# A recurrent attention and feed-forward kernel: the pipeline over batches shortened by one stage, with another slot order on every engine

## The reference

```python
q, k, v = split(LN(x) @ W_qkv.T)            # per head
k = (k - mean(k)) / sqrt(var(k) + eps)
F_t = retention * F_{t-1} + coef * outer(v_t, k_t)   # per head, 16x16, over the tokens
y_t = (W_LTM + F_t) @ q_t
x1 = x + LN(y @ W_o.T)
h = relu(LN(x1) @ W_fc.T) ** 2              # 1024 features
y = h @ W_proj.T
s = share of 5 steps in which a leaky integrator driven by y spikes
out = x1 + LN(s)
```

## Time and profile before

| | |
|---|---|
| median of 3 runs | 677.21 us (675.97 to 677.54) |
| the profiled execution: its own time | 680.4 us |
| its span, first to last instruction | 678.6 us |
| busy: TensorE, VectorE, ScalarE, GpSimd | 515.4, 544.6, 334.3, 384.4 us |
| mean granted TensorE clock | 0.888 |

### The profile page before, as it was taken

The page is one execution under the profiler, slowest core; times in us unless marked ns, Lnnn a source line. Parts: engine busy times, 40 slices in busy tenths (PEclk is TensorE's granted clock), DMA queues, the critical chain, the costliest instruction groups (busy, mean ns, idle before and its releaser), DMA issues.

```text
span 678.6 us, 7833 instructions
## 1 busy us (share of the span) xinstructions
PE 515.4 (76%) x2256; PEld 335.9 (49%) x2256; DVE 544.6 (80%) x1022; ACT 334.3 (49%) x633; POOL 384.4 (57%) x181
## 2 busy tenths in 40 slices
PE   0438458468998779878996979887978797797791
PEld 0224224234665357635764557545744573375570
DVE  4558999999899988997899789979998999911101
ACT  2423112334645654665556465665556534666734
POOL 0235765587558755865677556766577556812101
PEclk9999697777998889979898979987997899799796
DMA  6155654564455336544555454536353464020000
GB/s 222 46 155 149 173 174 148 149 185 139 131 158 178 125 116 179 172 138 116 179 161 136 112 176 127 175 88 190 126 148 116 148 178 125 0 64 0 0 32 31
DMA packets 54458, 87.64 MB, mean 129 GB/s; under 512 B 5392, under 2 KB 19088, under 8 KB 54416
## 3 DMA queue, kind: packets, MB, share of 16 engines
q1 hardware_dynamic: 54416, 87.14, 43.3%
HBM read 78.74 MB, written 8.39 MB: 128 GB/s over the span
## 4 chain that ended last, share of the span: by engine, by line
PE 34%; issue 23%; DVE 18%; ACT 15%; POOL 9%; DMA 1%; SPq 0%; POOLq 0%; DVEq 0%; ACTq 0%
DVE state L665 10%; PE p_c L378 9%; POOL prod L790 8%; PE p_c L351 7%; PE p_a L283 6%; DVE p_u L655 4%; ACT sign L529 4%; PE p_c L339 3%; PE p_y L326 3%; PE p_c L360 3%; ACT oo L456 2%; PE p_a L303 2%; ACT spk L456 2%; DVE stats L619 1%; ACT hr L517 1%
## 5 line engine op out<-in xcount | busy, mean ns | idle before, releaser
L790 POOL TENSOR_TENSOR prod<-state,qf 128x1024 f32<-128x1024 f32 x128 | 302.8, 2369 | 179.4 <-DVE state L665 167.3
L665 DVE TENSOR_TENSOR_SCAN state<-ret,p_u 128x512 f32<-128x512 f32 x256 | 307.8, 1208 | 0.0
L655 DVE TENSOR_TENSOR p_u<-vrep,p_k 128x512 f32<-128x512 f32 x256 | 171.6, 676 | 22.2 <-ACT p_k L461 22.1
L283 PE MATMUL p_a<-xt,wqkv_s 128*128 128x512 f32 x288 | 98.4, 487 | 39.4 <-POOL xt L806 15.3
L351 PE MATMUL p_c<-wproj_sb,ht 128*128 128x256 f32 x512 | 118.5, 383 | 1.3 <-ACT ht L519 1.3
L351 PEld LDWEIGHTS p_c<-wproj_sb,ht 128*128 128x128 f32 x512 | 94.9, 190 | 29.7 <-issue 10.0
L378 PE MATMUL p_c<-x1t,wfc_s 128*128 128x512 f32 x384 | 106.5, 429 | 3.6 <-POOL x1t L806 2.4
L283 PEld LDWEIGHTS p_a<-xt,wqkv_s 128*128 128x128 f32 x288 | 64.6, 235 | 78.8 <-issue 23.0
L378 PEld LDWEIGHTS p_c<-x1t,wfc_s 128*128 128x128 f32 x384 | 77.7, 206 | 31.4 <-issue 10.6
L326 PE MATMUL p_y<-prod,summer 128*32 128x512 f32 x512 | 78.6, 690 | 5.2 <-POOL prod L790 5.2
L517 ACT ACTIVATE hr<-p_c 128x512 f32<-128x512 f32 x64 | 38.1, 595 | 47.7 <-PE p_c L378 45.6
(11 more groups left out here) (88 smaller groups left out, 502.3 us busy)
## 6 DMA issues: line engine op xcount, KB each, us to landing
vrep<-v_rows SPq DMA_DIRECT2D x256, 256.0 KB, 3.4
xa<-in_x SPq DMA_DIRECT2D x8, 512.0 KB, 4.7
v_rows<-vf SPq DMA_DIRECT2D x16, 256.0 KB, 3.4
x<-in_x SPq DMA_DIRECT2D x8, 512.0 KB, 4.2
out<-x SPq DMA_DIRECT2D x8, 512.0 KB, 3.1
prod<-in_w_fc SPq DMA_DIRECT2D x1, 1024.0 KB, 7.2
wproj_sb<-in_w_proj SPq DMA_DIRECT2D x1, 1024.0 KB, 9.4
state<-in_w_qkv SPq DMA_DIRECT2D x1, 768.0 KB, 5.6
```

The costliest lines, as they stand in the source:

```text
L283: last = pe.matmul(p_a[:, :], wqkv_s[:, i, t, first_col:first_col + P], xt[:, j, t, :], start=(t == i == j == 0), stop=(t == KT - 1 and i ...
L655: v.tensor_tensor(p_u[n % NU][:, :], vrep[:, n % NV, :], p_k[:, :], ALU.mult).then_inc(S["hebb_done"], 1)
L665: v.tensor_tensor_scan(state[:, s % NS, i, :], ret[:, r:r + 1].broadcast_to([P, L]), p_u[n % NU][:, :], 0.0, ALU.mult, ALU.add).then_inc(S ...
L790: p.tensor_tensor(prod[:, s % NZ, :, :], state[:, s % NS, :, :], qf[:, s // HS, :].unsqueeze(1).broadcast_to([P, 2, L]), ALU.mult).then_in ...
```

## The change

One of the three trailing iterations is dropped, and with it the stage g - 3. All eight ups and downs 0 and 1 of batch g - 1 now stand in iteration g; downs 2 and 3, signs, count, norm 4 and the last residual of batch g - 2 too. `down` is issued whole. Of the removed lines of the four `iteration` bodies only a part is shown; the kernel above has them.

```diff
--- before.py
+++ after.py
             iteration(B, False, True, True, False)
             iteration(B + 1, False, False, True, False)
-            iteration(B + 2, False, False, False, False)
...
                 for s in range(SLOTS):
                     spread_v(g, s)
                     if s == 4: store_v(g, 1)
-                    if s == 6 and g >= 3: store_out(g - 3)
-                    if s == 8 and g >= 1: load_again(g - 1)
+                    if s == 2 and g >= 3: store_out(g - 3)
+                    if s == 5 and g >= 1: load_again(g - 1)
                     if s == 13 and g < B - 1: store_v(g + 1, 0)
                     if s == 12 and g < B - 2: load_x(g + 2)
...
 
 
             def project_out(b, t):
-                pe.wait_ge(S["relu_done"], at(FT * b - 1 + t))
+                pe.wait_ge(S["yf_done"], at(TILES * (b - 1) + 3 + t))
                 pe.wait_ge(S["y_done"], at(2 * (b + 1)))
 
-            def down(b, u, part, next_too):
-                if part == 0:
-                    if u < 2:
-                        if u == 0: pe.wait_ge(S["h_done"], at(FT * (b + 1)))
-                        if next_too: pe.wait_ge(S["o_done"], at(2 * (b + 1) + u + 1))
-                    else:
-                        pe.wait_ge(S["yf_done"], at(TILES * b + u - 1))
-                for f in range(part * FT // 2, (part + 1) * FT // 2):
+            def down(b, u):
+                if u == 0: pe.wait_ge(S["h_done"], at(FT * (b + 1)))
+                if u >= 2: pe.wait_ge(S["yf_done"], at(TILES * b + u - 1))
+                for f in range(FT):
                     last = pe.matmul(p_c[(u + 1) % 2][:, 0:D], ht[:, f, tokens(u)], wproj_sb[:, f, :],
                                      start=(f == 0), stop=(f == FT - 1))
-                if part == 1:
-                    last.then_inc(S["down_done"], 1)
+                last.then_inc(S["down_done"], 1)
             def count_spikes(b, pair, next_too):
                 pe.wait_ge(S["sign_done"], at(2 * b + pair + 1))
                 if next_too: pe.wait_ge(S["x1t_done"], at(KT * (b + 1) + pair + 1))
+                else: pe.wait_ge(S["yf_done"], at(TILES * b + 3 + pair))
             def turn_x1(b, t):
                 pe.wait_ge(S["n3_done"], at(TILES * (b + 1)))
                 pe.wait_ge(S["o_done"], at(2 * (b + 1)))
-                pe.wait_ge(S["yf_done"], at(TILES * (b - 1) + 3 + t))
...
             def iteration(g, now, before, two_before, after):
                 b, b1, b2 = g + 1, g - 1, g - 2
                 for s in range(SLOTS):
-                    if before and s in (0, 2): sums(b1, 6 + s // 2)
+                    if before and s in (0, 1): sums(b1, 6 + s)
                     if now and s >= 4 and s % 2 == 0: sums(g, (s - 4) // 2)
...
                     if now:
                         if s == 0: project_v(g, 1)
                         if s == 1: project_k(g, 1)
                         if s == 2: key_variance(g, 1)
...
+                    if two_before and s in (0, 1): down(b2, 2 + s)
+                    if before and s == 2:
+                        project_out(b1, 0)
+                        project_out(b1, 1)
+                    if now and s == 3: project_q(g, 1)
                     if now and s == 5: key_scale(g, 1)
...
                     if after:
                         if s in (6, 7): turn_x(b, s - 6)
                         if s == 9: project_v(b, 0)
                         if s == 10: project_k(b, 0)
                         if s == 11: key_variance(b, 0)
...
+                        if s == 12: project_q(b, 0)
+                        if s == 13: key_scale(b, 0)
+                    if before and s == 8:
+                        turn_x1(b1, 0)
+                        turn_x1(b1, 1)
+                    if two_before and s == 9:
+                        count_spikes(b2, 0, before)
+                        count_spikes(b2, 1, before)
+                    if before and 9 <= s < 13:
+                        up(b1, 2 * (s - 9))
+                        up(b1, 2 * (s - 9) + 1)
+                    if before and s in (13, 14): down(b1, s - 13)
 
             run(iteration)
 
...
             nc.scalar.copy(wfc_s[:, 0, :, :], wfc_raw).then_inc(S["wide_high"], 1)
 
             def iteration(g, now, before, two_before, after):
...
+                b, b1, b2 = g + 1, g - 1, g - 2
                 for s in range(SLOTS):
...
+                    if s == 0:
+                        if now and before: copy_key(g, 0)
+                        if two_before: copy_yf(b2, 1)
+                        if now: copy_v(g, 1)
+                        if two_before: signs(b2, 0)
+                    if s == 1:
+                        if now: square_k(g, 1)
+                        if two_before: copy_yf(b2, 2)
+                    if s == 2:
+                        if before: copy_y(b1, 1)
+                        if two_before: copy_yf(b2, 3)
+                        if now: key_deviation(g, 1)
+                        if after: deviation(1, b)
+                        if before:
+                            copy_o(b1, 0)
+                            copy_o(b1, 1)
+                    if s == 3:
+                        if now: copy_q(g, 1)
+                        if after: norm1(b)
+                        if before: deviation(2, b1)
+                    if s == 4:
+                        if now: spread_k(g, 1)
+                        if before: norm(2, b1, oo, oo, "x1_done", b1)
+                    if two_before and s == 5: signs(b2, 1)
+                    if s == 6:
+                        if after: copy_xt(b, 0)
+                        if before: deviation(3, b1)
+                    if s == 8:
+                        if now: copy_key(g, 1)
+                        if after: copy_xt(b, 1)
+                        if before:
+                            norm(3, b1, x1[b1 % 2], oo, "x1_done", b1 + 1)
+                            copy_x1t(b1, 0)
+                            copy_x1t(b1, 1)
                     if after and s == 9: copy_v(b, 0)
...
+                    if two_before and s == 9:
+                        copy_count(b2, 0)
+                        copy_count(b2, 1)
+                    if after and s == 10: square_k(b, 0)
                     if now and s == 11: copy_y(g, 0)
...
+                    if after and s == 11: key_deviation(b, 0)
                     if after and s == 12:
                         copy_q(b, 0)
                         spread_k(b, 0)
...
+                    if two_before and s == 12: deviation(4, b2)
+                    if before and 9 <= s < 13:
+                        hidden(b1, 2 * (s - 9))
+                        hidden(b1, 2 * (s - 9) + 1)
+                    if two_before and s == 13: norm(4, b2, spk, spk, "res_done", b2)
+                    if before and s == 14: copy_yf(b1, 0)
 
             run(iteration)
 
...
             dve.wait_ge(S["tables_done"], 1)
 
             def iteration(g, now, before, two_before, after):
-                b, b1, b3 = g + 1, g - 1, g - 3
+                b, b1, b2 = g + 1, g - 1, g - 2
                 for s in range(SLOTS):
                     first = s % HS == 0
                     if now and not first: hebbian(g, s, 0)
                     if s > 0 and now: scan(g, s - 1, 1)
                     if s == 0 and before: scan(b1, SLOTS - 1, 1)
-                    if b3 >= 0 and s == 0: statistics(4, b3, spk, "spk_done", 2 * (b3 + 1))
-                    if before and s == 8: scales(2, b1)
+                    if after and s == 0: statistics(1, b, xa, "x_in", 16 * (b + 1))
                     if now:
                         if first: hebbian(g, s, 0)
                         hebbian(g, s, 1)
                         scan(g, s, 0)
-                    if after and s == 2: statistics(1, b, xa, "x_in", 16 * (b + 1))
-                    if b3 >= 0 and s == 1: scales(4, b3)
+                    if after and s == 2: scales(1, b)
+                    if before and s == 3: statistics(2, b1, oo, "o_done", 2 * (b1 + 1))
                     if now and s == 4: key_reciprocal(g, 1)
+                    if before and s == 4: scales(2, b1)
                     if now and s == 6: norm_k(g, 1)
-                    if after and s == 4: scales(1, b)
-                    if before and s == 6: statistics(2, b1, oo, "o_done", 2 * (b1 + 1))
-                    if before and s == 10: statistics(3, b1, x1[b1 % 2], "x1_done", b1 + 1)
-                    if before and s == 11: scales(3, b1)
+                    if before and s == 6: statistics(3, b1, x1[b1 % 2], "x1_done", b1 + 1)
+                    if before and s == 7: scales(3, b1)
+                    if two_before and s == 11: statistics(4, b2, spk, "spk_done", 2 * (b2 + 1))
                     if after and s == 12: key_reciprocal(b, 0)
+                    if two_before and s == 13: scales(4, b2)
                     if after and s == 14: norm_k(b, 0)
 
             run(iteration)
...
```

(8 more changed lines are left out.)

63 lines of the change are left out of this document (removed).

## The result

The changed kernel takes 706.44 us (median of 4 runs, 702.01 to 707.76), the kernel before beside it 676.59 (4 runs, 675.18 to 677.54). The ratio is 1.041, 95% interval 1.037 to 1.045: slower, by 27.7 us if the ratio is taken and by 29.9 between the two medians. The prediction was 711 us in 690 to 728, slower with a chance of 0.90. The profiled execution took 705.96 us with a span of 704.1, 25.5 more than the 678.6 of before (whose profiled execution, 680.4 us, was itself one of the longer ones; that makes the difference of the spans smaller than that of the medians).

What follows compares the result with a forecast made beforehand. A loop through TensorE, ScalarE, VectorE and GpSimd was to bind: 75.1 us, 76.3 with the low clock. Attention output at 649.3 plus a 63.5 tail gave 712.8, 711 on the median, 80% range 690 to 728.

Steps and rivals of the forecast that it cites:

- a: TensorE in order without a hole, from up 0 to the key variance in the next iteration: 40.8 us.
- b: ScalarE makes the key deviation, then norm 1's deviation, for which VectorE waits in slot 2: 0.7 us.
- c: VectorE from scales 1 in slot 2 through slots 3 to 7 to scales 3: 23.4 us.
- d: From there until x1t is complete, through VectorE's scan in slot 9, GpSimd's read and two lows: 10.2 us.
- The second path through project_out: Longer on TensorE and with a copy, but past scales 1 and slot 3: 74.4 us against 75.1.
- The sum: Attention output of batch 7 at 649.3 us plus 63.5 behind it: end at 712.8, 711 on the median.
- the clock: TensorE's low clock after the hole of slots 4 to 9 delays up 0 by 1.2 us, 1.6 in the first round.
- The tail: From the attention output of batch 7 to the end: 63.5 us where before it was 71.1.
- A: Rival: VectorE binds and nothing stalls, 642 us or 640 on the median; chance 0.08.
- B: Rival: the loop comes out at about today's 71.7 us, 684 on the median, up to 694; chance 0.09.
- C: Rival: the clock stays low into the ups in every round, period 79.5, about 730 us; chance 0.08.
- The parts costed at nothing: store_out and load_again earlier on SyncE, and project_out's added wait for the copies of downs 2 and 3: no cost.

Runs made afterwards that it cites:

- both extra-work kernels: Changed kernel with down 3's sixteen matmuls issued once more on TensorE, in slot 1 or in slot 4: 730.9 us (1.079) and 704.2 us (1.040).
- the repeat: The changed kernel run once more without any edit: 705.53 us, ratio 1.040 to the kernel before.
- four of the kernels with a shorter stretch a): Changed kernel with downs 2 and 3 in slot 4, 689.12 us; that plus filler, 682.38; down 3 in slot 4, down 2 behind project_k, 685.22; GpSimd's reads freed, 682.18.
- one and two downs moved: Changed kernel with down 3, or downs 2 and 3, moved to TensorE's slot 4: 703.58 us (1.037) and 689.12 us (1.015).
- the keys early: Against the kernel with downs 2 and 3 in slot 4: next batch's key chain ahead of the ups, deviation 4 ahead of spread_k; 690.51 us (1.019).
- the last two: Changed kernel with the keys early, down 0 in slot 13, down 1 in slot 1, downs 2, 3 in slot 4: 692.75 us; then GpSimd's reads freed: 682.18.
- The eight useless matmuls: Added between project_k and the key variance to the kernel with downs 2 and 3 in slot 4: 682.38 us (1.006) against 689.12.

## Why the prediction was right

**The loop, term by term.** From up 0 at 380.32 to the end of the key variance at about 421.2, 40.9 us (a: predicted 40.8). From there to scales 1 at 421.77, 0.6 (b: 0.7). From scales 1 to norm 3, which ScalarE starts at 445.30, 23.5 (c: 23.4). From there to up 0 at 455.52, 10.2 (d: 10.2). Sum 75.2 against 75.1. The loop was laid out in series from rows of before alone, since no operation is new. The order of the queues says which stand in series, and both extra-work kernels confirm it: the added 3.5 us came back as 3.4 in the loop and as 0 outside. Two readings of the prediction are loose and harmless: the terms of step d) add up to 10.1 and not to 10.2, and the 13.5 and 12.0 us of step b) are counted from two different moments. In the trace VectorE was ready for scales 1 at 417.49, 12.0 us after 405.5, and down 1 ended 2.8 later than that (408.31); this is why the wait is 4.3 us and not 1.5.

**VectorE's waits.** Predicted 4, 2 and 3 us in slots 2, 12 and 13; measured 4.28, 1.97 and 2.78. The second path through project_out, at 0.7 us below the first: measured, with scales 1 moved out of the way that path gives a period of 75.36 (343.56 to 418.92), so the two are nearer than I had them and bind together. VectorE's waits from iteration 0 to the last scan add up to 66.6 us where I had said about 75, and the last scan ends at 626, not near 633; both follow from the size of the sum, which comes next.

**The sum.** Up to the attention output of batch 7 I had 649.3; measured is 643.08, 6.2 too much. Up 0 of the first round came 2.2 earlier than my x1t (150.92 for 153.1), and this is a difference of two larger errors, so that it was luck that it is so small. VectorE began iteration 0 at 42.33, 2.05 earlier than before (44.38), since the key variance and the projection of q ahead of it took 1.06 and 1.76 us where they took 1.88 and 2.93 before: the same instructions at another clock, no step of the change. Then scales 1 waited 3.16 us where I had 5.4. That made it 4.2 us early, and at scales 1 of iteration 1 it still was (115.32 for 119.5). Behind that came a wait which the prediction did not have (TensorE's and VectorE's timelines):

```profile
114.63 6.12 PE L338 MATMUL p_c<-wo_sb,yt 128*128 128x256 f32 x16
...
121.46 1.41 DVE L613 BATCH_NORM_STATS2 stats<-oo 128x6 f32<-128x256 f32 x4 [1.92 <-ACT oo L448]
```

project_out of iteration 1, which I had costed at 3.6 us, took 6.12 at the low clock, and VectorE waited 1.92 for it.

The six rounds took 454.35 for my 457.7, and from the last up 0 to the output 37.8 for 38.5. These 4 us are one mis-sized term, the clock. I had 1.2 us in each round, 1.6 in the first (its 76.8 has 0.1 more than that), and 1.2 behind the last. The first cost more than that, 78.5 against 75.1 without clock; TensorE's timeline of the changed kernel there:

```profile
150.92 5.49 PE L372 MATMUL p_c<-x1t,wfc_s 128*128 128x512 f32 x12 [2.29 <-POOL x1t L800]
```

The same two ups take 3.06 at 380.32; the sums behind them and the counts at the end of the round are 0.3 and 0.5 longer than there. The other rounds cost 0.5 down to 0, where I had 1.2. The low clock itself is there as forecast, 24 us of each iteration, and project_v and the counts do run at it. I had put their excess ahead of up 0, but they end just as x1t is complete: their time lies beside GpSimd's read and lows, which is step d). That cover stood in my own step, and I counted both. The Trainium skill, "TensorE: Matmul & The Clock Gate", Part 1: The HAM clock gate, puts the ramp penalty under 1% of a span; the trace of the changed kernel agrees, with 3.4 + 0.5 + 0.2 + 0.1 in the rounds and 1.9 in iteration 1, some 6 us in 704. Its sum, 3 us below mine, would have been the nearer one.

**Iteration 0.** Scales 1 was to wait 5.4 us; it waited 3.16 in the profiled execution and 5.24 in the repeat. TensorE's timeline of the profiled one:

```profile
52.00 1.67 PE L282 MATMUL p_a<-xt,wqkv_s 128*128 128x512 f32 x6 [0.73 <-ACT vf L448]
```

And of the repeat:

```profile
50.45 2.93 PE L282 MATMUL p_a<-xt,wqkv_s 128*128 128x512 f32 x6 [0.73 <-ACT vf L448]
```

The projection ahead of the key variance ran at the high clock in the one and at the low clock in the other. The forecast took the low one from the earlier trace rows, so the clock of iteration 0 is a term that one execution does not fix.

**The tail.** Predicted 63.5, measured 61.0. From the output to x1t complete at 660.80 it is 17.7 (17.4). Of the count at the low clock (1.3) only 0.1 is left, up 0 at 660.86: it ran beside GpSimd's lows, the same oversight as in the loop. Ups and the last hidden take 12.8 (12.7 + 1.35, so I had 1.3 too much for slow ups), and from the first down to the end it is 30.5 (30.7).

**The rivals.** A (VectorE binds, 640 us) asked for a stretch a) shorter by 9 us; it was 40.9 and VectorE waits 34.5 us more than before. The rule beside it, of the Trainium skill, "Perfetto Trace Analysis", Identifying the Most-Contended Engine, to improve the engine with the highest occupancy, is not borne out here: VectorE is still the fullest at 77%, and 3.5 us an iteration of extra work on TensorE, at 72%, moved the end by 25. B (684 us) is not what happened, but it is where four of the kernels with a shorter stretch a) arrived, 682 to 689. C (730 us) was seen in the first round alone, and there only in part (two ups slow); in the five others twelve matmuls of ups took 3.05 to 3.15 us. The parts costed at nothing held: the SyncE steps by experiment, project_out's new wait by its row, which starts at once behind the key variance (421.09).

**Where my expectations failed** was behind the prediction, in the repairs. Each time I took the next bound from the kernel at hand and did not walk the new loop to its end as I had done for the change. Five kernels came out 17 to 46 us above what was expected (one and two downs moved, the keys early, and the last two; spans). The causes, each with a row above: a clock hole ahead of project_out, GpSimd's reads behind ups, and work in front of up 0.

## What to carry to other kernels

Dropping a pipeline stage can make work of two iterations into one loop that runs through the queues of in-order engines. Walk it once around in series, in the new order, and compare it with the busy time of the fullest engine: the longer one is the least that the period can be. Put the same useless work into two places of a schedule: where the time grows by its full length is the loop, where it grows by nothing is slack. Only work that leaves the first kind of place can gain. When work leaves the loop, look at what stands there instead, a wait, a low clock behind it, another engine's buffer that now comes free later.

## What the runs showed of the hardware that was not expected

A short hole before cheap work cost more than a long one. TensorE spent 24 us of each iteration at the low clock in its half-empty stretch and that cost 0.2 us on the loop in the iteration shown, while a wait of 1.18 us before eight matmuls of 128x8 put the sixteen matmuls behind it at 5.39 us instead of 3.70, and one of 2.17 us at up to 6.72. With 0.30 to 0.47 us of wait there they took 3.69 to 3.70. The wait alone does not settle it: in iteration 1 of the kernel with the keys early, a wait of 1.17 us stood in the same place, and project_out took 3.70. The eight useless matmuls that closed the hole in most part made the whole kernel 6.7 us faster, so in this kernel work that nobody needs was worth its time.

The same order of instructions met the clock in different phases: iteration 0 of two executions of the changed kernel differed by 2.1 us in one wait (3.16 and 5.24), and iterations of the kernel with the keys early took 72.3 to 72.5 and 74.5 to 74.6 us in turn, with project_out at 6.5 to 6.7 and at 5.39 us in turn.
